# Transformer layers on one core: batches numbered through both layers instead of an outer loop over layers

## The reference

```python
def _layer(x, wqkv, qs, ksc, wo, lg, lb, w1, b1, w2, b2):
    h = shift_token(x)                      # second half of the features comes from the token before
    q, k, v = jnp.split(h @ wqkv, 3, axis=-1)
    q = l2norm(q) * qs;  k = l2norm(k) * ksc
    q, k = rotary_xpos(q, k)
    o = local_attention(q, k, v)            # windows of 128 tokens, each sees itself and the one before
    x = x + o @ wo
    h = shift_token(x)
    h = (h - mu) / jnp.sqrt(var + 1e-05) * lg + lb
    a, g = jnp.split(h @ w1 + b1, 2, axis=-1)
    h = a * jax.nn.gelu(g, approximate=False)
    return x + h @ w2 + b2
```

## Time and profile before

| | us |
|---|---|
| median of 3 runs | 4021.46 (4021.03 to 4022.46) |
| the profiled execution's own time | 4024.32 |
| its span, first to last instruction | 4022.5 |
| mean granted TensorE clock | 0.954 of full speed |
| busy: PE / DVE / ACT / POOL | 3525.9 / 2649.0 / 2150.1 / 1524.5 |

### The profile page before, as it was taken

One profiled execution on the slowest core, in us unless ns is written; L12 is line 12 of the kernel. 1 busy time (PEld: TensorE's weight loads), 2 busy tenths in 40 slices (PEclk: granted clock), 3 DMA queues, 4 the chain that ended last, 5 costly groups with the idle time before them and its releaser, 6 DMA issues.

```text
span 4022.5 us, 74042 instructions
## 1 busy us (share of the span) xinstructions
PE 3525.9 (88%) x26976; PEld 2106.8 (52%) x26976; DVE 2649.0 (66%) x4194; ACT 2150.1 (53%) x2586; POOL 1524.5 (38%) x1584
## 2 busy tenths in 40 slices
PE   2888888888866899999999999758999999999999
PEld 1223323232224566766667666526666676667666
DVE  4778778787744677666766675355667666776664
ACT  0656565656533455556555555333555555555554
POOL 1111112121014355554455454234444554555443
PEclk7999999999977899999999999878999999999999
DMA  2222222322120000110011001200100110001101
GB/s 55 49 58 57 53 58 53 67 46 64 38 76 6 22 25 23 34 35 25 23 34 33 27 23 29 79 16 9 36 25 23 34 34 26 23 23 34 36 19 35
DMA packets 157747, 147.50 MB, mean 37 GB/s; under 512 B 11676, under 2 KB 156112, under 8 KB 157648
## 3 DMA queue, kind: packets, MB, share of 16 engines
q1 hardware_dynamic: 157648, 146.17, 13.6%
HBM read 78.79 MB, written 33.55 MB: 28 GB/s over the span
## 4 chain that ended last, share of the span: by engine, by line
issue 36%; POOL 25%; PE 7%; DVE 2%; POOLq 1%; ACT 0%; DMA 0%; DVEq 0%; SPq 0%; ACTq 0%
POOL f_u L1424 6%; POOL f_u L1429 6%; POOL f_hT_l L1440 4%; POOL f_Pl L1448 3%; POOL f_xb L1456 2%; POOL f_Pl L1450 2%; PE f_p L978 1%; PE f_p L1059 1%; PE f_p L1078 1%; POOL f_mark_l L1445 1%; POOL f_qst L1434 1%; PE f_p L1100 1%; DVE f_negm L1310 0%; PE f_p L1004 0%; POOLq L1444 0%
## 5 line engine op out<-in xcount | busy, mean ns | idle before, releaser
L650 DVE TENSOR_REDUCE m_negm<-m_p 128x2 f16<-128x1024 f32 x512 | 608.7, 1222 | 169.9 <-PE m_p L469 168.1
L572 ACT ACTIVATE m_Pr<-m_p 128x1024 f32<-128x1024 f32 x512 | 500.5, 1020 | 163.7 <-PE m_p L488 159.3
L1424 POOL TENSOR_TENSOR f_u<-f_u,f_bt 128x1024 f32<-128x1024 f32 x128 | 302.1, 2360 | 612.4 <-DVE f_bt L1282 612.4
L1059 PE MATMUL f_p<-f_vl,f_Pl 128*128 128x65 f32 x3584 | 430.2, 280 | 16.4 <-POOL f_Pl L1450 16.4
L1059 PEld LDWEIGHTS f_p<-f_vl,f_Pl 128*128 128x128 f32 x3584 | 418.5, 196 | 27.6 <-issue 26.7
L1181 ACT ACTIVATE f_Pl<-f_p 128x896 f32<-128x896 f32 x256 | 220.4, 914 | 329.3 <-PE f_p L1045 219.9
L1440 POOL TENSOR_TENSOR f_hT_l<-f_hp,f_hT_h 128x512 f16<-128x512 f32 x192 | 222.0, 1156 | 409.3 <-ACT f_hp L1204 408.1
L978 PE MATMUL f_p<-f_wq_h,f_xT_h 128*128 128x512 f16 x768 | 296.5, 386 | 75.3 <-DVE f_mark_x L1268 47.3
L497 PE MATMUL m_o<-m_Pr,m_vm 128*32 128x512 f32 x2048 | 341.4, 645 | 12.9 <-ACT m_Pr L572 12.9
L1196 ACT ACTIVATE f_G<-f_p,f_bias 128x512 f32<-128x512 f32 x192 | 131.4, 685 | 347.6 <-PE f_p L1100 347.6
L1310 DVE TENSOR_REDUCE f_negm<-f_p 128x4 bf16<-128x1024 f32 x256 | 295.9, 1223 | 15.4 <-PE f_p L1011 15.4
(11 more groups left out here) (222 smaller groups left out, 7839.8 us busy)
## 6 DMA issues: line engine op xcount, KB each, us to landing
f_xs<-out SPq DMA_DIRECT2D x32, 512.0 KB, 4.8
f_xr<-out SPq DMA_DIRECT2D x32, 512.0 KB, 4.4
f_xh<-attn_res SPq DMA_DIRECT2D x32, 512.0 KB, 3.9
out<-f_xb SPq DMA_DIRECT2D x32, 512.0 KB, 3.2
m_xin<-in_L_attn_x SPq DMA_DIRECT2D x16, 512.0 KB, 3.9
out<-m_xn SPq DMA_DIRECT2D x16, 512.0 KB, 3.0
m_QT<-m_hi SPq DMA_DIRECT2D x128, 64.0 KB
m_KT<-m_hi SPq DMA_DIRECT2D x128, 64.0 KB
```

Of the source, the lines that this page charges most:

```text
L572: act.activation(Pr[kt % 2][:, 2 * u:2 * u + 2, :].rearrange("p h t -> p (h t)"), psum[w.slot("M2", g, kt, u)][:, :], ACT.Exp).then_inc(*w ...
L650: dve.tensor_reduce(negm[:, t, pr // 2, :, pr % 2], psum[w.slot("M1", h, u)][:, :].rearrange("p (a k) -> p a k", a=2), AX.X, ALU.max, nega ...
L1059: mm = pe.matmul(psum[w.slot("PV", hp)][:, e * T + t * (DH + 1):e * T + (t + 1) * (DH + 1)], Pl[h % 4][:, at * W:(at + 1) * W], vl[:, j, h ...
L1424: pool.tensor_tensor(u[t][:], u[t][:], bt[:], ALU.add).then_inc(*bt_used.up(I))
```

## The change

The outer loop and the section `weights` are gone. An `Inst` now has a `base` (layer x 16), and batches are numbered 0 to 31, with layer 1's batches 16 to 31; `I.local` is the number within the layer. The sections are: `queries`; for each layer `first`, `second`, `third`, `rounds` (the loop) and `tail` (C of its last batch, N of the one before, F of the one before that); at the end `late` and `last`. In layer 1 `first` also holds N of batch 15 and F of batch 14, and `second` also F of batch 15; these were in layer 0's `last`.

The step WB is cut into five:
- WQ: `wqkv` and the tables, staged in `u0` to `u2`, with `wo`'s load behind them (staged in `u3`). For layer 0 in `queries`. For layer 1 SP issues the loads at the start of `tail`, ACT makes `wq_h` after C.LM, DVE `wq_l` and the tables after F.W1, and PE waits for `wq_l` at the tail's end.
- WO_: `wo_h` and `wo_l`. For layer 0 at the start of `first`, for layer 1 at the end of layer 0's `tail`; PE waits for it at the end of `first`.
- WE: the load of `b2`, on SP at the end of `second`.
- WF: the loads of `w1`, `ln_b`, `ln_g`, `b1`, `w2` on SP at the start of `third`, after a hold until the layer before is stored; after LM in `third` the 48 matmuls on PE, `w2_h` and `w1_h` on ACT, and on DVE `w2_l`, the bias, the scaling, `w1_l` and a memset. `w1` is staged in both halves of `hT`, `w2` in the gelu buffers.
- WR: PE's wait for all low parts, at the end of `third`.

ZB, and the load of `ar` for it, run in layer 1 alone, as a plain addition. The loads of `xs` in layer 1 hold for the store of that batch in layer 0.

```diff
-            I.local = I.b
+            I.local = I.b - I.base if I.base else I.b
...
+        return Inst(f"{name}{layer}", 0, add, base=layer * B)
+
+    def weave(name, **late):
+
+        at, layer = name
+        return woven(order, **{x: of(f"{x}_{at}_", (layer if n >= 0 else layer - 1), (lambda i, n=n: layer * B + n)) for x, n in late.items()})
+
+    def with_steps(steps, engine, where, *new):
+
+        old = steps[engine]
+        at = {"start": 0, "end": len(old)}.get(where)
...
+            at = 1 + max(n for n, step in enumerate(old) if step[0] == where)
+        steps[engine] = old[:at] + list(new) + old[at:]
+
+    K = [Inst(f"K{layer}", 0, (lambda i, layer=layer: layer)) for layer in range(L)]
+    sections = [Section("queries", {engine: [("WQ", K[0])] for engine in ENGINES})]
+    for layer in range(L):
+        more = layer > 0
+        r0 = weave(("first", layer), A=0, **(dict(N=-1, F=-2) if more else {}))
+        r1 = weave(("second", layer), A=1, C=0, **(dict(F=-1) if more else {}))
+        r2 = weave(("third", layer), A=2, C=1, N=0)
+        if not more:
+            for engine in ("ACT", "DVE"):
+                with_steps(r0, engine, "start", ("WO_", K[0]))
+        with_steps(r0, "PE", "end", ("WO_", K[layer]))
+        with_steps(r1, "SP", "end", ("WE", K[layer]))
+        with_steps(r2, "SP", "start", ("WF", K[layer]))
+        for engine in ("PE", "ACT", "DVE"):
+            with_steps(r2, engine, "LM", ("WF", K[layer]))
+        with_steps(r2, "PE", "end", ("WR", K[layer]))
+        sections += [Section(f"first{layer}", r0), Section(f"second{layer}", r1), Section(f"third{layer}", r2)]
+        v = layer * B
+        sections.append(Section(f"rounds{layer}", woven(order, A=of("A", layer, lambda i: i), C=of("C", layer, lambda i: i - 1),
+                                                        N=of("N", layer, lambda i: i - 2), F=of("F", layer, lambda i: i - 3)),
+                                loop=(v + 3, v + B)))
+        tail = weave(("tail", layer), C=B - 1, N=B - 2, F=B - 3)
+        if layer < L - 1:
+            with_steps(tail, "SP", "start", ("WQ", K[layer + 1]))
+            for engine, where in (("ACT", "LM"), ("DVE", "W1")):
+                with_steps(tail, engine, where, ("WQ", K[layer + 1]))
+                with_steps(tail, engine, "end", ("WO_", K[layer + 1]))
+            with_steps(tail, "PE", "end", ("WQ", K[layer + 1]))
+        sections.append(Section(f"tail{layer}", tail))
+    sections += [Section("late", weave(("late", L - 1), N=B - 1, F=B - 2)), Section("last", weave(("last", L - 1), F=B - 1))]
...
+        U = sb("u", [P, NT, 2 * INNER], F32)
+        u = [U[:, t, :] for t in range(NT)]
...
+        st_q = U[:, 0:NT - 1, :].rearrange("p t n -> p (t n)").rearrange("p (c n) -> p c n", c=NC)
+        st_o = u[NT - 1].rearrange("p (f n) -> p f n", f=NP_)
+        st_1 = hT[:].rearrange("p a f t -> p (a f t)").bitcast(F32)[:, 0:NC * 2 * HID].rearrange("p (c n) -> p c n", c=NC)
+        st_2 = gates[:].rearrange("p a t -> p (a t)")[:, 0:NF * D].rearrange("p (f n) -> p f n", f=NF)
...
+            def wq(I):
+                pe.wait_ge(*w_lo.at(I, 1))
+
+            def wo_weights(I):
+                pe.wait_ge(*w_lo.at(I, 2))
+
+            def wf(I):
+                pe.wait_ge(*w1_loaded.at(I, w1_loaded.per))
...
+            def wr(I):
+                pe.wait_ge(*w_lo.at(I, 4))
...
-                act.activation(wo_h[:], st_o, ACT.Copy, scale=WSCALE).then_inc(*w_hi.up(K))
+            def wq(I):
+                act.wait_ge(*wq_loaded.at(I, wq_loaded.per))
+                act.activation(wq_h[:], st_q, ACT.Copy, scale=WSCALE).then_inc(*w_hi.up(I))
+
+            def wo_weights(I):
+                act.wait_ge(*wo_loaded.at(I, wo_loaded.per))
+                if I.b > 0:
+                    act.wait_ge(*x1_ready.at(all_of_layer(I.b), 0))
+                act.activation(wo_h[:], st_o, ACT.Copy, scale=WSCALE).then_inc(*w_hi.up(I))
...
+            def wf(I):
+                act.wait_ge(*w2_loaded.at(I, w2_loaded.per))
                 act.activation(w2_h[:, 0:NF - 1, :], st_2[:, 0:NF - 1, :], ACT.Copy, scale=WSCALE)
-                act.activation(w2_h[0:TAIL, NF - 1, :], st_2[0:TAIL, NF - 1, :], ACT.Copy, scale=WSCALE).then_inc(*w_hi.up(K))
...
-                act.wait_ge(*w_lo.at(K, 4))
-                act.wait_ge(*tables_done.at(K, 4))
+                act.activation(w2_h[0:TAIL, NF - 1, :], st_2[0:TAIL, NF - 1, :], ACT.Copy, scale=WSCALE).then_inc(*w_hi.up(I))
...
+            def wq(I):
+                dve.wait_ge(*w_hi.at(I, 1))
+                dve.scalar_tensor_tensor(wq_l[:], st_q, WSCALE, wq_h[:], ALU.mult, ALU.subtract).then_inc(*w_lo.up(I))
...
+            def wo_weights(I):
+                dve.wait_ge(*w_hi.at(I, 2))
+                dve.scalar_tensor_tensor(wo_l[:], st_o, WSCALE, wo_h[:], ALU.mult, ALU.subtract).then_inc(*w_lo.up(I))
+
+            def wf(I):
+                dve.wait_ge(*w_hi.at(I, 3))
                 dve.scalar_tensor_tensor(w2_l[:, 0:NF - 1, :], st_2[:, 0:NF - 1, :], WSCALE, w2_h[:, 0:NF - 1, :],
...
-                                         ALU.mult, ALU.subtract).then_inc(*w_lo.up(K))
-                dve.wait_ge(*tables_loaded.at(K, tables_loaded.per))
-
-                for i in range(2):
...
+                                         ALU.mult, ALU.subtract).then_inc(*w_lo.up(I))
+                dve.wait_ge(*w1_loaded.at(I, w1_loaded.per))
                 dve.wait_ge(*w.is_full("WB"))
...
+                dve.tensor_tensor(w1_l[:], st_1, w1_h[:], ALU.subtract).then_inc(*w_lo.up(I))
+                dve.wait_ge(*w_lo.at(I, 4))
+                dve.memset(hT_h[:, NF - 1, :], 0.0)
 
...
             def zb(I):
-
+                if I.base < (L - 1) * B:
+                    return
                 dve.wait_ge(*xb_ready.at(I, 1))
-                dve.wait_ge(*ar_loaded.at(I, 16))
-                dve.scalar_tensor_tensor(xb[:].rearrange("p t d -> p (t d)"), ar[:].rearrange("p t d -> p (t d)"), is_last[:, 0:1],
-                                         xb[:].rearrange("p t d -> p (t d)"), ALU.mult, ALU.add).then_inc(*z_ready.up(I))
+                dve.wait_ge(*ar_loaded.local(I, 16))
+                dve.tensor_tensor(xb[:].rearrange("p t d -> p (t d)"), ar[:].rearrange("p t d -> p (t d)"),
+                                  xb[:].rearrange("p t d -> p (t d)"), ALU.add).then_inc(*z_ready.up(I))
...
-                dve.wait_ge(*z_ready.before(I, 1))
+                if I.base == (L - 1) * B:
+                    dve.wait_ge(*z_ready.local(I, 0))
...
-                dve.wait_ge(*z_ready.at(I, 1))
+                if I.base == (L - 1) * B:
+                    dve.wait_ge(*z_ready.local(I, 1))
+                else:
+                    dve.wait_ge(*xb_ready.at(I, 1))
...
             def ls(I):
+                pool.wait_ge(*b2_loaded.at(weights_of(I), 16))
...
+            def wq(I):
+                layer = I.b
+                if layer > 0:
+                    hold(hi_ready.at(all_of_layer(layer), 0))
+                    hold(q_lo_ready.at(all_of_layer(layer), 0))
+                    hold(stack_ready.at(all_of_layer(layer), 0))
                 sp.wait_ge(const_done, N_CONST)
-                def load(done, dst, src):
-                    sp.dma_start(dst, src, allow_slow_non_contiguous=True).then_inc(*done.up(K, 16))
-                load(wq_loaded, st_q, wqkv[layer].rearrange("(c p) n -> p c n", p=P))
+                load(I, wq_loaded, st_q, wqkv[layer].rearrange("(c p) n -> p c n", p=P))
...
+                load(I, tables_loaded, qk_scale[:, 1, :], k_scale[layer].partition_broadcast(P))
+                load(I, wo_loaded, st_o, wo[layer].rearrange("(c p) n -> p c n", p=P))
+
+            def we(I):
+                hold(xb_ready.at(all_of_layer(I.b), 0))
...
+            def wf(I):
+                layer = I.b
+                hold(y_stored.at(all_of_layer(layer), 0))
...
-                    load(w1_loaded, st_1[:, c, :], w1[layer][c * P:(c + 1) * P, :])
...
+                load(I, w2_loaded, st_2[:, 0:NF - 1, :], w2[layer][0:(NF - 1) * P, :].rearrange("(f p) n -> p f n", p=P))
...
             def xt(I):
                 hold(xT_ready.before(I, 1))
+                if I.base:
+                    hold(y_stored.before(I, B))
                 sp.dma_start(xs[:], out_v[I.local]).then_inc(*x_loaded.up(I, 16))
...
             def xh_(I):
+                if I.base < (L - 1) * B:
+                    return
```

157 lines of the change are left out of this document (58 added, 99 removed).

## The result

The changed kernel takes 3974.84 us (median of 4 runs, 3972.86 to 3976.53), the kernel before 4021.4 beside it. The ratio is 0.9884, 95% interval 0.987 to 0.9899. The forecast was 3973. Its profiled execution has a span of 3972.9 us, 49.6 less than before, and a mean granted clock of 0.960 instead of 0.954.

A forecast was written before the change was run, and what follows sets the result against it. The prediction took PE to bound the loop rounds and something else, such as weight staging, the layers' edges. Its terms summed to -48.2 us, 4024.32 to 3976.1 for the profiled execution, 3973 as a median, range about 3950 to 3990.

The forecast's parts named there:

- The start, -16.4: Start of layer 0: PE waits only for `wq_h` and `wq_l`, so the first XT eviction comes at 1172.9, not 1189.29.
- so it is there: Start of layer 0: `xs`, behind six loads of some 0.4 us of queue each, has arrived when PE needs it.
- `third`, +18.6 twice: `third` of each layer: RN waits behind WF on DVE, including 9.5 us of bias matmuls; the round is 18.6 us later.
- the rival of the cheap matmuls: Both `third` sections: bias matmuls at full clock or hidden, 4 us less in each, 3965 in all; chance 0.20.
- The tail, +3.5: `tail` of layer 0: `wq_h` on ACT, `wq_l` and four table products on DVE add 3.5 us, between 0 and 7.8.
- The turn, -76.1: Turn of the layers: the 141.1 us from batch 15's WO to batch 17's XT eviction become 65.
- The term for LS: `first` of layer 1: LS on POOL, 2.35 us long, adds 2.4 to the 65 us of the turn.
- `second`, +1.6: `second` of layer 1: with F of batch 15 added, it grows from 81.4 to a loop round of 82.04, plus 1.
- `late`, +2: `late`: W1,0 of batch 30 gets WO's slot and waits for DVE's eviction, 2 us more, between 0 and 2.5.
- The loop rounds, 0: The 26 loop rounds: same order of steps and slots, so no change; far end -0.4 a round, -10 in all.
- The first section that doesn't overlap: Rival for `first` of layer 1: A's and F's chains run one after the other, 78.4 instead of 65, total 3986; chance 0.12.

The follow-up runs named there:

- e_nomm: The changed kernel with 2 of the 48 recorded bias matmuls left in each `third`, everything else the same: 3968.16 us.
- e_wq: The changed kernel with `wq_h` moved behind the second pair of exponentials and `wq_l` and the tables behind PV,0 in layer 0's tail: 3967.86 us.
- e_ls: The changed kernel with LS of batch 15 moved to POOL's end of `first` in layer 1: 3971.06 us.
- e_serial: The changed kernel without overlap at the turn: layer 0's last N and F run before layer 1's `first`, weights still staged early: 4020.4 us.
- e_rn: The changed kernel with RN ahead of DVE's part of WF in both `third` sections, `w1_l` behind LN, `w1_h` behind the first exponentials: 3964.2 us.

## Why the prediction was right, and which terms were not

- **What bounds the kernel.** PE in the rounds, waits at the edges: right. The rounds stayed within 0.2 us of 82.03, and all but 4.2 us of what moved, moved at the edges.
- **The start, -16.4.** -14.6. Of the weights only `wq_l` gates XT, as said, but "so it is there" of `xs` was wrong: its load ended PE's wait, 0.91 us behind `wq_l`, which costs 0.7. The other 1.1 come from `wq_h`, which started at 1165.63 instead of 1164.56; DVE was done with the first phase 0.9 later too.
- **`third`, +18.6 twice.** Mechanism right: RN late by 17.8 and the section by 16.9 and 15.6. The matmuls were priced right for layer 0 (9.48 for 9.53) and too high for layer 1 (8.20), where the rival of the cheap matmuls was partly true. `w2_h` and `w2_l` cost nothing, as said, but only because they stood in the same gap as the matmuls: e_nomm shows that without the matmuls they come last, and that RN then gains 5.5 us. The 48 are the trace's records of 24 matmuls; no sum changes by it.
- **The tail, +3.5.** From mark 15 to the end of WO it took 148.2 before (2530.71 less 2382.48) and 155.0 after: +6.8. The forecast was an estimate between 0 and 7.8, and mis-sized. It priced the table products beside an idle POOL; here the four took 4.2 us instead of 1.4. e_wq won back 5.9 of it up to mark 16.
- **The turn, -76.1.** -71.6 (69.5 us instead of 65). The term for LS was its length, 2.35, without what it waits for. The row that it priced LS from, at 2519.92, is of batch 14; LS of batch 15, with its wait of 8.62, stood in the same trace. In a loop round that store is done when POOL comes to LS (no LS there has idle before it, in either kernel); in this section, without the work of C, F of 14 ends only just ahead, and POOL's order made batch 16 wait for it. e_ls gave 4.6 of it back.
- **`second`, +1.6, and `late`, +2.** +0.6 and -0.2. The wait for the slot of WO did come, 1.41 us, but it was covered: XH of batch 31 starts 172.9 us after that batch's mark in both kernels. PE in `late`:

```profile
3914.88 0.38 PE L1145 MATMUL f_p<-f_xhT_h,f_w_h 128*128 128x512 f16 x1 [1.41 <-DVE f_x L1389]
```

- **The loop rounds, 0.** -4.2 over 24 distances; the forecast had named up to -10 as an end. Its cause stays open.
- **The rivals.** The first section that doesn't overlap was worked out at 78.4 and would have come to 3986; it was 69.5 us long, a third of the way there. e_serial puts a price on full failure: the whole gain.

The errors have both signs and cancel: 1.8, 1.0 and 7.8 us too optimistic, 1.7, 2.2, 1.0, 3.0, 2.0 and 2.2 too pessimistic. That the total came out within 1.4 us is therefore in part luck; the table by stage, and not the total, shows which terms held.

## What to carry to other kernels

Weight preparation that is taken off the edge of a pipeline has to be put behind the steps for which other engines wait; set ahead of them it costs in the fill what it saved at the edge (in this kernel, e_serial: 36.4 us won, 33.7 paid, 4020.4 for 4021.4). When a step moves, price the semaphore it waits for at the new place and who is queued behind it, not its duration alone. And put one mark in each round of the trace and compare stage by stage, since the total hides errors that cancel.

## What the runs showed of the hardware that was not expected

- One kernel (e_rn) took 3984 us in one execution and 3964 to 3969 in the others. Two of them were profiled, and there most of the difference is the level of TensorE's clock in two sections of 88 to 101 us: the same 56 matmuls took 12.21 us at a granted clock of 0.50, or 6.89 at 0.95. Idle times of 9.73 and 5.61 us came ahead of the slow ones, 5.07 and 4.62 ahead of the fast ones.
- Small operations of DVE took over three times their usual length while POOL worked beside them: 1.37 and 1.51 us for table products of 0.41, with the two H1 of POOL at 4.43 for 2.31. The Trainium skill ("SBUF — State Buffer", section "SBUF: two separate sides") has the two engines share a pair of ports that one of them holds for a whole instruction, if the DVE operation has two inputs in SBUF and the GpSimd one reads SBUF; these do, and 0.41 with the 1.16 of one H1 makes 1.57, near to what they took. The rows agree; no run here tested it alone.
